# Layer 0's attentions in a two-layer Perceiver kernel: three norms scaled by ScalarE, part of the work moved between the engines

## The reference

```python
x = x + xattn(layernorm(x), ctx)       # cross attention to ctx
x = x + attn(layernorm(x))             # self attention, 16 heads of 8, rotary in layer 0
x = x + ffn(layernorm(x))              # experts: top 1 with capacity in layer 0, top 2 in layer 1
# layer 0's cross attention, one head of 128:
scores = (q @ k.T) / sqrt(128); keep the 32 largest of 257; softmax; @ v; @ Wo.T + bo
# layernorm: (x - mean) / sqrt(var + 1e-5)
```

## Time and profile before

| | |
|---|---|
| median of 3 runs | 1766.65 us (1763.15 to 1766.8) |
| the profiled execution | 1764.01 us, its span 1762.2 us, mean granted clock 0.943 |
| layer 0's attentions | to about 399 us |
| PE busy over the span | 1531.9 us (87%) |
| DVE | 1113.5 us (63%) |
| ACT | 841.5 us (48%) |
| POOL | 516.0 us (29%) |

### The profile page before, as it was taken

The page is one execution under the profiler, slowest core; times in us unless marked ns, Lnnn a source line. Parts: engine busy times, 40 slices in busy tenths (PEclk is TensorE's granted clock), DMA queues, the critical chain, the costliest instruction groups (busy, mean ns, idle before and its releaser), DMA issues. The chain is left out here.

```text
span 1762.2 us, 46064 instructions
## 1 busy us (share of the span) xinstructions
PE 1531.9 (87%) x15634; PEld 1159.3 (66%) x15634; DVE 1113.5 (63%) x3480; ACT 841.5 (48%) x2372; POOL 516.0 (29%) x1099
## 2 busy tenths in 40 slices
PE   4888888876859839999999999969999999499998
PEld 2666666655547626666666666657777777388887
DVE  3899999956400127777777777756666666433333
ACT  2444444421223227777777777734444344144443
POOL 1333333320530434444444444422222222000000
PEclk9999999975879959999999999989999999799999
DMA  5444522200111111111111111000000000000000
GB/s 177 141 146 146 194 96 96 96 2 1 39 52 53 41 41 34 33 33 35 34 33 33 33 33 36 24 1 1 0 0 0 0 0 0 1 7 12 6 12 12
DMA packets 56815, 76.27 MB, mean 43 GB/s; under 512 B 5816, under 2 KB 44356, under 8 KB 56640
## 3 DMA queue, kind: packets, MB, share of 16 engines
q1 hardware_dynamic: 54720, 72.08, 13.4%
q0 software_dynamic: 2048, 3.58, 0.7%
HBM read 67.47 MB, written 8.78 MB: 43 GB/s over the span
## 5 line engine op out<-in xcount | busy, mean ns | idle before, releaser
L1592 ACT ACTIVATE c_pr<-c_pS,c_nm 128x257 f32<-128x257 f32 x512 | 238.6, 472 | 97.8 <-DVE c_nm L1726 97.8
L1726 DVE TENSOR_REDUCE c_nm<-c_pS 128x1 f32<-128x257 f32 (+1 forms) x384 | 173.3, 506 | 42.9 <-PE c_pS L1472 42.6
L1476 PE MATMUL c_pT<-cst,c_pr 128*128 128x128 f32 x1024 | 163.2, 284 | 0.0
L1966 ACT ACTIVATE s_k<-s_pK 128x512 f32<-128x512 f32 x128 | 76.5, 598 | 176.8 <-PE s_pK L1893 176.8
L1346 ACT ACTIVATE f_hid<-f_pH,vec 128x512 f32<-128x512 f32 x128 | 88.1, 688 | 127.9 <-PE f_pH L1308 126.8
L1368 DVE SCALAR_TENSOR_TENSOR X<-f_pY,f_mk,X 128x128 f32 x256 | 72.1, 344 | 111.5 <-PE f_pY L1318 111.5
L1893 PEld LDWEIGHTS s_pK<-s_hT,AH 128*128 128x128 f32 x1024 | 123.6, 194 | 25.9 <-ACT s_k L1966 22.8
L1893 PE MATMUL s_pK<-s_hT,AH 128*128 128x128 f32 x1024 | 137.3, 283 | 0.5 <-ACT s_hT L1961 0.5
L1476 PEld LDWEIGHTS c_pT<-cst,c_pr 128*128 128x128 f32 x1024 | 111.3, 141 | 37.7 <-issue 37.7
L1318 PEld LDWEIGHTS f_pY<-f_w,f_hid 128*128 128x128 f32 x1024 | 122.3, 192 | 5.0
L1318 PE MATMUL f_pY<-f_w,f_hid 128*128 128x128 f32 x1024 | 124.1, 276 | 0.0
(11 more groups left out here) (300 smaller groups left out, 3319.4 us busy)
## 6 DMA issues: line engine op xcount, KB each, us to landing
a_ctxT<-in_ctxT SPq DMA_DIRECT2D x32, 514.0 KB, 3.7
c_ctxT<-in_ctxT SPq DMA_DIRECT2D x128, 128.5 KB, 2.2
a_ctxN<-in_ctxR SPq DMA_DIRECT2D x32, 512.0 KB
f_w<-in_f_w SPq DMA_DIRECT2D x16, 256.0 KB, 5.4
rows_in<-a_zero SPq DMA_DIRECT2D x7, 320.0 KB, 5.9
f_h<-rows_in SPq DMA_DIRECT2D x7, 320.0 KB, 3.3
rows_out<-f_y SPq DMA_DIRECT2D x7, 320.0 KB, 2.4
f_w<-in_f_w SPq DMA_DIRECT2D x16, 128.0 KB, 5.3
```

Of the source, the lines that this page charges most:

```text
L1476: mm = pe.transpose(pT[:, c, j, :], pr[:, b % 2, j, c * P:(c + 1) * P], k("ident"))
L1592: act.activation(pr[:, b % 2, c, :], pS[:, c, 0:S], ACT.Exp, bias=nm[:, c:c + 1], accum_out=den[:, b % 2, c:c + 1]).then_inc(e_ready.sem, 1)
L1726: dve.tensor_reduce(nm[:, c:end], pS[:, c:end, 0:S], AX.X, ALU.max, negate=True).then_inc(max_ready.sem, 1)
```

## The change

The norm's scale moves from DVE to ACT as `rstd * x + shift`, and POOL forms `shift = -mean * rstd` in one more instruction. ACT does the three scales in its own order: w and z between its scores and `normed_z`, u last. The masks, sums and the last token are done in another way:

- The last token: no `prL`, its transpose or L407. DVE adds `ctxL * weight` to the sums when it takes them from PSUM (`sums_with_last`), and ACT then scales that. `ctxL` is loaded once for each of the four batches, broadcast to 32 partitions.
- The self values: the mask stands in the weights (`avq`, built once by POOL), so ACT copies them out. Four columns of ones stand beside them (`vq` has 4 x 36 columns a batch), so that `self_sums` gives the sums of the exponentials as well, and `self_weight_sums` is gone.
- The bias: POOL adds it to X before (`add_bias`), and DVE adds the output in one step.
- The tiles in the bank `pO` are laid out anew, and DVE's order is changed.

```diff
@@ class Norm
+    def gpsimd_again(self, pool, r):
+        if not (isinstance(r, int) and r == 0):
+            pool.wait_ge(self.h_ready.sem, self.h_ready.at(r - 1))
+            carry(pool, self.ctx)
+        self.gpsimd(pool, r)
+        self.gpsimd_shift(pool, r)
+    def gpsimd_shift(self, pool, r):
+        pool.wait_ge(self.rstd_ready.sem, self.rstd_ready.at(r))
+        carry(pool, self.ctx)
+        pool.tensor_scalar(self.shift[:, :], self.mv[:, 0:1], self.rstd[:, :], -1.0, ALU.mult, ALU.mult).then_inc(self.shift_ready.sem, 1)
+    def scalar_scale(self, act, x, r):
+        act.wait_ge(self.shift_ready.sem, self.shift_ready.at(r))
+        act.activation(self.h[:, :], x, ACT.Identity, bias=self.shift[:, :], scale=self.rstd[:, :]).then_inc(self.h_ready.sem, 1)
...
@@ sync
-                    sp.wait_ge(u_done.sem, u_done.at(g - 2))
+                    sp.wait_ge(cs_ready.sem, cs_ready.at(g - 2))
...
-                sp.dma_start(ctxL[:, p, :], io["ctxL"][bass.ds(g * BG, BG), :]).then_inc(ctxN_loaded[p].sem, 16)
+                for b in range(BG):
+                    sp.dma_start(ctxL[b * T:(b + 1) * T, p, :], io["ctxL"][bass.ds(g * BG + b, 1), :].broadcast_to([T, D])
+                                 ).then_inc(ctxN_loaded[p].sem, 16)
@@ tensor
             pe.wait_ge(router_loaded.sem, 16)
+            pe.wait_ge(av_spread.sem, HQ)
...
-                turn(pU[0:BG, SC, :], prL[:, :]).then_inc(pT_done.sem, 1)
...
-                pe.matmul(pU[:, 3, :], prLT[:, :], ctxL[:, p, :], start=False, stop=True,
-                          skip_group_check=True).then_inc(u_done.sem, 1)
...
-                        mm = pe.matmul(pO[b * T:(b + 1) * T, 0, c * T:(c + 1) * T], seT[:, c, b * T:(b + 1) * T],
-                                       vq[:, b, c * T:(c + 1) * T], start=True, stop=True)
+                        mm = pe.matmul(pOs[b * T:(b + 1) * T, c, :], seT[:, c, b * T:(b + 1) * T], vq[:, b, c, :], start=True, stop=True)
@@ scalar, slot
                 run(queries, x)
+                run(self_values, a)
                 run(exponentials, t)
                 run(queries_by_keys, x)
                 run(scores, x)
+                run(scale_w, w_)
+                run(scale_z, z)
                 run(normed_z, z)
                 run(self_exponentials, a)
-
+                run(scale_u, u)
@@ gpsimd, slot
+                run(norm_w, w_)
+                run(add_bias, x)
                 run(spread_keys, a)
+                run(norm_z, z)
+                run(norm_u, u)
                 run(keep, z)
@@ vector
+            def sums_with_last(u, p, r):
+                dve.wait_ge(ctxN_loaded[p].sem, ctxN_loaded[p].at(r - 1))
+                dve.wait_ge(u_done.sem, u_done.at(u))
                 dve.wait_ge(p_ready.sem, p_ready.at(u))
+                dve.scalar_tensor_tensor(cs[:, :], ctxL[:, p, :], pr[:, SM:S], pU[:, 3, :], ALU.mult, ALU.add).then_inc(cs_ready.sem, 1)
@@ vector, slot
                 run(largest(0), t)
-                run(last_weights, u)
                 run(inverse_sum, u)
                 run(mark(0), t)
-                run(self_weight_sums, z)
                 run(largest(1), t)
...
                 run(mark(1), t)
+                run(lambda u: sums_with_last(u, p, r), u)
+                run(rotate, a)
                 run(self_inverse_sums, z)
-                run(rotate, a)
...
-                run(self_values, a)
-                run(scale_w, w_)
                 run(add_self_output, z)
-                run(add_bias, u)
                 run(rows_z, z)
                 run(add_output, u)
...
                 run(self_maxima, a)
-                run(scale_z, z)
                 run(self_below_max, a)
-                run(lambda g: n2.vector_scale(dve, x_of(g), g), u)
```

More of the change, by code:

```diff
@@ L176, in __init__ @@
         self.stats, self.mv, self.ve, self.rstd = f("stats", [P, 6]), f("mv", [P, 2]), f("ve", [P, 1]), f("rstd", [P, 1])
-        self.h = f("h", [P, D])
+        self.h, self.shift = f("h", [P, D]), f("shift", [P, 1])
+        self.shift_ready = Signal(ctx, nc, f"{name}_shift_ready")
         self.stats_ready = Signal(ctx, nc, f"{name}_stats_ready")
@@ L200, in gpsimd, with vector_rows_again, vector_moments_again @@
         pool.tensor_tensor(self.rstd[:, :], self.ve[:, :], self.env["k"]("half"), ALU.pow).then_inc(self.rstd_ready.sem, 1)
+    def vector_rows_again(self, dve, x, r):
+        if not (isinstance(r, int) and r == 0):
+            dve.wait_ge(self.mv_ready.sem, self.mv_ready.at(r - 1))
+            carry(dve, self.ctx)
+        self.vector_rows(dve, x)
+    def vector_moments_again(self, dve, r):
+        if not (isinstance(r, int) and r == 0):
+            dve.wait_ge(self.shift_ready.sem, self.shift_ready.at(r - 1))
+        self.vector_moments(dve, r)
+    def gpsimd_again(self, pool, r):
+        if not (isinstance(r, int) and r == 0):
+            pool.wait_ge(self.h_ready.sem, self.h_ready.at(r - 1))
[9 more added lines that the diff above has]
+        act.activation(self.h[:, :], x, ACT.Identity, bias=self.shift[:, :], scale=self.rstd[:, :]).then_inc(self.h_ready.sem, 1)
     def vector_scale(self, dve, x, r, out=None):
@@ L227, in attend_layer0 @@
         ctxT = sb("ctxT", [P, 2, BG, S])
-        ctxL = sb("ctxL", [BG, 2, D])
+        ctxL = sb("ctxL", [P, 2, D])
         wr = sb("router", [P, E])
@@ L254, in attend_layer0 @@
         ctxT_loaded = [sig(f"ctxT_loaded{p}", 16) for p in range(2)]
-        ctxN_loaded = [sig(f"ctxN_loaded{p}", 32) for p in range(2)]
+        ctxN_loaded = [sig(f"ctxN_loaded{p}", 16 * (1 + BG)) for p in range(2)]
         hT_done, hT_ready = sig("hT_done"), sig("hT_ready")
@@ L507, in _, with x_of, scale_w, scale_u @@
         def _(act):
+            def x_of(g):
+                return X[:, bass.ds(g, 1), :].rearrange("p g d -> p (g d)")
+            def scale_w(w_):
+                if later(w_):
+                    act.wait_ge(hT_done.sem, hT_done.at(w_ - 1))
+                n1.scalar_scale(act, x_of(w_), w_)
+            def scale_u(u):
+                n2.scalar_scale(act, x_of(u), u)
+            def scale_z(z):
+                if later(z):
+                    act.wait_ge(h3_kept.sem, h3_kept.at(z - 1))
+                n3.scalar_scale(act, x_of(z), z)
             def normed_x(x):
@@ L534, in turned_weights @@
                 act.activation(prT[:, :, :], pU[:, 0:SC, :], ACT.Copy).then_inc(pT_ready.sem, 1)
-                act.activation(prLT[:, :], pU[0:BG, SC, :], ACT.Copy).then_inc(pT_ready.sem, 1)
             def sums(u):
                 act.wait_ge(rinv_ready.sem, rinv_ready.at(u))
-                act.wait_ge(u_done.sem, u_done.at(u))
-                act.activation(cu[:, :], pU[:, 3, :], ACT.Copy, scale=rinv[:, :]).then_inc(u_ready.sem, 1)
+                act.wait_ge(cs_ready.sem, cs_ready.at(u))
+                act.activation(cu[:, :], cs[:, :], ACT.Copy, scale=rinv[:, :]).then_inc(u_ready.sem, 1)
             def turned_sums(u):
@@ L559, in turned_self_weights, with self_values @@
                 act.wait_ge(seT_done.sem, seT_done.at(z))
-                act.activation(seT[:, :, :], pO[:, :, :], ACT.Copy).then_inc(seT_ready.sem, 1)
+                act.activation(seT[:, :, :].rearrange("p c t -> p (c t)"), pO[:, :], ACT.Copy).then_inc(seT_ready.sem, 1)
+            def self_values(a):
+                act.wait_ge(vq_done.sem, vq_done.at(a))
+                act.activation(vq[:, :, :, 0:HQ * HD], pQ[:, 1, :].rearrange("p (b c e) -> p b c e", b=BG, c=NQ), ACT.Copy
+                               ).then_inc(vq_ready.sem, 1)
             def turned_self_sums(z):
                 act.wait_ge(oT_done.sem, oT_done.at(z))
-                act.activation(oT[:, :], pO[:, 1, :], ACT.Copy).then_inc(oT_ready.sem, 1)
+                act.activation(oT[:, :], pO[:, 144:272], ACT.Copy).then_inc(oT_ready.sem, 1)
             def normed_z(z):
@@ L568, in normed_z @@
                 act.wait_ge(h3T_kept.sem, h3T_kept.at(z, 0))
-                act.activation(h3T[:, :], pO[:, 3, :], ACT.Copy).then_inc(h3T_ready.sem, 1)
+                act.activation(h3T[:, :], pO[:, 0:P], ACT.Copy).then_inc(h3T_ready.sem, 1)
             def slot(w_, x, t, u, a, z, l, p, r):
@@ L583, in slot @@
                 run(scores, x)
+                run(scale_w, w_)
+                run(scale_z, z)
                 run(normed_z, z)
                 run(self_exponentials, a)
+                run(scale_u, u)
+            scale_w(0)
             slots(act, slot)
@@ L592, in _, with add_bias, norm_w, norm_u @@
             n1.gpsimd(pool, 0)
-            pool.memset(zero[:, :], 0.0).then_inc(zeroed.sem, 1)
+            n1.gpsimd_shift(pool, 0)
+            pool.memset(avq[:, :, :, :, :], 0.0).then_inc(av_zeroed.sem, 1)
+            pool.wait_ge(av_zeroed.sem, 1)
+            for h in range(HQ):
+                pool.tensor_copy(avq[:, h, :, h, :], w("av").rearrange("p (c h d) -> p c h d", h=HQ, d=HD)[:, :, h, :]).then_inc(av_spread.sem, 1)
```

(19 more changed lines are left out.)

94 lines of the change are left out of this document (42 added, 52 removed).

## The result

The changed kernel takes 1845.35 us (median of 4 runs, 1844.21 to 1846.56) against 1766.72 before: 1.0448 times as long, 95% interval 1.0429 to 1.0466. Forecast were 1834 us, with a range of 1779 to 1858 and a chance of 0.87 for slower. The span grew by 82.4 us, from 1762.2 to 1844.6.

The account below looks back on a forecast made before the run. The prediction took DVE as the bound, with a ring of waits through PE, DVE and ACT of 10.35 us just behind. 1764.0 us + 68 in 30 slots + 2 in the drain = 1834 us, range 1779 to 1858.

Parts of the forecast that it names:

- the ring: Loop slot's cycle through PE, DVE and ACT, from `a_se` over `a_nmax` to the next `a_se`; 10.35 us before.
- the spread keys: POOL's bias addition makes `spread_keys` end some 0.7 us later, still before PE's scores must run.
- DVE stops being the bound: In layer 0's attentions DVE alone would need 8.8 us a slot; an ordinary slot took 10.54 before.
- The ring grows to 11.14 us at the full clock: PE-DVE-ACT cycle goes from 10.35 to 11.14 us, ends 10.6 and 12; ACT's end of the slot adds 0.90.
- The rows that I took: Each scale on ACT priced as `a_u` and `a_vT`, 0.37 us at 128x128, with ends of 0.25 and 0.63.
- The other edits: `a_prL` transpose and `ctxL` passes gone -0.52 us, self sums' 36 columns +0.11, last token's term on DVE +0.06.
- Falls in nearly every slot at 2.0 us: PE's thin part grows from 2.8 to about 4.3 us; the granted clock falls, costing 2.0 us, slot 13.14.
- +68 us in 30 slots: 30 slots of layer 0's attentions at 13.14 us in place of 10.86 add 68 us.
- +2 in the drain: Draining slots have the shift and a scale more in their path, 0.5 us each: +2 us.
- POOL is no bound: POOL's 4.03 us a slot grow by three shifts and an addition to at most 6.2 of 11.
- Rival B: The ring grows, clock falls as seldom as before or every third slot at most; 1782 or 1792 us; chance 0.27.
- Rival C: Faster: scales lie in ACT's free time, 0.90 and 0.24 drop out, the ring is 10.0 us; 1748 us; chance 0.08.

Follow-up runs that it names:

- e3: The changed kernel with 10 unread matmuls a slot in PE's waits; ratio 1.0117 to the kernel before.
- e11: The kernel before with three unread 128x128 ACTIVATEs on ACT ahead of `normed_z`; ratio 1.0268 to the kernel before.
- e1: The changed kernel with its three scales back on DVE, all other edits kept; ratio 1.0018 to the kernel before.
- e10: e9 with POOL's bias behind `spread_keys`, one unread matmul ahead of the self scores and two ahead of the scores; ratio 0.9885 to the kernel before.
- e7: e1 with three unread matmuls ahead of the scores on PE; ratio 0.9906 to the kernel before.
- e4: The kernel before with three unread matmuls ahead of the scores on PE; ratio 0.9934 to the kernel before.
- e9: e7 with `scale_w` on ACT ahead of the exponentials, DVE's fourth mark earlier, unread matmuls ahead of the self scores; ratio 0.9943 to the kernel before.

## Why the prediction was right

The mechanism was the one forecast, a longer ring and a lower clock on top of it, and the time was 11 us above the forecast. That it came so near is in part luck: in the 30 slots the ring was priced 19 us too low and the clock 8 us too high. One step was wrong, the spread keys (below).

- *DVE stops being the bound*: it was busy 8.34 of 13.33 us, 63%.
- *The ring grows to 11.14 us at the full clock*: right in kind, too small. e3 has 11.75 on average and 11.8 in its usual slots. One of them, 233.65 to 245.43:

```profile
233.65 0.14 DVE L734 TENSOR_SCALAR a_nmax<-a_top 128x1 f32<-128x1 f32 x1
...
237.31 0.62 ACT L614 ACTIVATE a_se<-a_sd 128x512 f32<-128x512 f32 x1
...
238.53 0.60 PE L405 MATMUL a_pO<-cst,a_se 128*128 128x128 f32 x4
...
240.64 0.90 PE L503 MATMUL a_pO<-a_vq,a_seT 128*32 128x36 f32 x32
...
241.86 0.33 PE L405 MATMUL a_pU<-cst,a_u 128*128 128x128 f32 x1 [0.33 <-ACT a_u L598]
...
245.43 0.14 DVE L734 TENSOR_SCALAR a_nmax<-a_top 128x1 f32<-128x1 f32 x1
```

  In this slot each group of unread matmuls ends before the result that PE needs next can be used, so the slot is the ring. Its three pieces, each with its forecast: `a_nmax` to `a_se` 3.66 (3.36), `a_se` to its transposes 1.22 (1.09), from there to the next `a_nmax` 6.90 (351.89 - 344.85 - 0.35 = 6.69). Together 11.78 for 11.14, so each piece holds a mis-sized term:
  - A scale on ACT lasts 0.48 us and not 0.37. The rows that I took have one operand with a value per partition (a scale or a bias); this one has both, and it reads SBUF. `a_u`, which now reads SBUF with a scale alone, takes 0.40, and e11's three, from SBUF with neither, take 0.30 each. So most of the 0.11 goes with the second operand and some 0.03 with the source; the two functions differ as well (Copy and Identity), and no run takes them apart:

```profile
L228 ACT ACTIVATE a_n_h<-X,a_n_shift,a_n_rstd 128x128 f32 (+1 forms) x96 | 43.6, 482 | 10.4 <-POOL a_n_shift L224 10.4
L589 ACT ACTIVATE a_u<-a_cs,a_rinv 128x128 f32<-128x128 f32 x32 | 12.8, 401 | 69.8 <-DVE a_cs L739 69.8
```

  - `a_nmax` to `a_sc` was taken as 1.67 from a draining slot; in a full slot it is 251.22 - 249.38 = 1.84, and it was that before the change too.
  - The other edits take 0.14 off the last piece and not 0.35. PE waits 0.33 us for `a_u` where 0.06 was summed; the self sums of 36 columns last 0.90 like those of 32, where 0.11 more was summed; and DVE's neighbours cost more (L190 waits 0.26 behind L791, not 0.16). The same step fails e1's theory: its usual slot of 10.50 has 6.94 in this piece.
- *Falls in nearly every slot at 2.0 us*: right, the price a little high. The slots lost 405.0 - 352.4 = 52.6 us, 1.75 each.
- *+68 us in 30 slots*: 79.3, of which the ring 35 (forecast 16) and the clock 44 over what it cost before (forecast 52).
- *+2 in the drain*: 1.4. The start, taken as 0, is 2.0 us shorter; what follows the attentions is 3.6 us longer. Cut into stretches of 97 us from 400.24 and from 479.00, it has the same PEclk before and after in all but one, from 1467 and from 1546: 0.89 before, 0.84 after. PE's busy time over the 10642 passes grew by the same 3.6 us (1218.8 to 1222.4). Why the clock stood lower there no run tells, and 3.6 us lie within what the runs of one kernel spread.
- *POOL is no bound*: its shift took 0.29 us and its bias 0.46, and no scale waited for a shift in an ordinary slot. But that the spread keys come before PE must run was wrong: PE waits 0.80 us for them at the self scores. The prediction counted 0.8 us of waiting ahead of the scores; most of it now lies one step earlier, for the keys, and 0.17 is left for `q2`. In the changed kernel nothing hangs on it, since `a_sd` is done 1.2 us before `a_se` starts; in the faster ones 0.2 us a slot does (e10).
- Rival B, which the Trainium skill's rule stood beside ("TensorE: Matmul & The Clock Gate", section "HAM oscillation — how this bites in real kernels"), did not come: from 48 to 426 us no wait of PE is longer than 1.44 us, and the clock fell in almost every slot. The measurement decides against long idle gaps as the only cause.
- Rival C, faster, comes only without the scales on ACT and with the clock held up (e7): 0.9%, of which about 0.7% is the clock, as e4 shows. The 0.3% left for the other edits is not shown by the ratios, whose intervals overlap; the traces have 313.7 us for e7's slots and 317.1 for e4's.

The estimate by the Trainium skill, "ScalarE: Activation LUTs", section "Rules for kernel authors", 0.41 us for an ACTIVATE with a bias per partition, was nearer than my row but still short of 0.48.

## What to carry to other kernels

Where an engine looks like the bound, look for a slot that lacks some of its work: if little time comes back, a ring of waits stands right behind, and an instruction that a change puts into that ring lengthens every slot, however idle its engine is over the slot. Taking 18% off the busiest engine bought nothing here, and three instructions of 0.48 us on an engine busy for half the time cost 1.2 us a slot at the full clock, and 1.5 more by the clock. So a wait on TensorE can cost twice, once as time and once through the granted clock in the work behind it; unread matmuls in its waits show which part is the clock's, and must themselves stay out of the ring.

## What the runs showed of the hardware that was not expected

- An ACTIVATE of 128x128 took 0.48 us from SBUF with a scale and a bias per partition, 0.40 from SBUF with a scale alone, 0.36 to 0.37 from PSUM with one of them, and 0.30 from a constant tile with neither; three of the last kind, which waited for nothing, took 0.70 together.
- PE's granted clock fell in nearly every slot of the changed kernel, though PE's longest wait from 48 to 426 us was 1.44 us; with matmuls that nobody read in those waits the slots read 1.00, 2.4 GHz. Three unread matmuls a slot left three slots of 12.1 us in e9 and none in e10, where they are placed otherwise and the keys come earlier. How much waiting a slot can bear before the clock falls, no run here shows.
- A shorter ring can give nothing: 11.46 and 11.75 us at the full clock became 13.47 and 13.50 unfilled.
- The kernel before itself became 0.66% faster by matmuls that nobody reads.
